# Experts of a routed layer as products of high and low parts, split tile by tile on ACT and DVE

## The reference

```python
x = L0_attn_hidden_states                      # 1 x 2048 x 512
x = x + L0_attn(layernorm(x))                  # Mamba-2 mixer, then a gated dense layer (2048 wide)
x = x + L0_ffn(layernorm(x))                   # routed experts

# _L0_ffn_ref: 8 experts of width 352, the 2 best of each row
probs = softmax(x @ Wr);  topk_w, topk_idx = top_k(probs, 2);  topk_w /= sum(topk_w)
g = einsum('bsh,ehi->besi', x, Wg)
u = einsum('bsh,ehi->besi', x, Wu)
h = silu(g) * u
y = einsum('besi,eih->besh', h, Wd)
out = einsum('bse,besh->bsh', combine, y)
```

## Time and profile before

| | us |
|---|---|
| median of 3 runs (lowest, highest) | 1515.2 (1514.8, 1515.47) |
| the profiled execution | 1515.05 |
| its span in the trace | 1513.3 |
| PE busy | 1439.8 |
| DVE busy | 782.0 |
| ACT busy | 446.9 |
| POOL busy | 431.4 |

### The profile page before, as it was taken

How to read it: one execution, slowest core, us unless ns; L and a number is a source line. 1 busy time by engine, 2 the same in 40 slices (tenths; PEclk the granted TensorE clock), 3 DMA queues, 4 the chain that set the end, 5 groups by cost and what they waited for, 6 DMA issues and landing times.

```text
span 1513.3 us, 19850 instructions
## 1 busy us (share of the span) xinstructions
PE 1439.8 (95%) x6903; PEld 1059.0 (70%) x6903; DVE 782.0 (52%) x1258; ACT 446.9 (30%) x927; POOL 431.4 (29%) x457
## 2 busy tenths in 40 slices
PE   6799999799999997999999999999988999999996
PEld 5577778566666666888888888888867655655663
DVE  6968787689999993332333333333468322222221
ACT  4445444545555553211111121112121111111110
POOL 2512121247777753111011011101010233332331
PEclk9899999999999999999999999999999999999998
DMA  9122223722233216001000000120377233333322
GB/s 197 56 92 103 85 84 132 209 91 98 105 113 125 98 57 209 28 15 43 14 28 23 19 28 14 48 70 0 109 249 247 45 61 66 67 59 67 61 40 34
DMA packets 84354, 124.41 MB, mean 82 GB/s; under 512 B 27695, under 2 KB 44079, under 8 KB 84272
## 3 DMA queue, kind: packets, MB, share of 16 engines
q1 hardware_dynamic: 71488, 103.62, 21.1%
q0 software_dynamic: 8736, 18.62, 7.2%
q10 hardware_dynamic: 4048, 1.10, 0.3%
HBM read 81.37 MB, written 43.78 MB: 83 GB/s over the span
## 4 chain that ended last, share of the span: by engine, by line
PE 59%; DVE 1%; DMA 1%; issue 0%; ACT 0%; POOL 0%; POOLq 0%; ACTq 0%; DVEq 0%
PE fin_bank L1797 35%; PE fin_bank L1938 12%; PE fin_bank L1958 6%; PE fin_bank L1928 1%; PE fin_bank L1907 1%; PE fin_bank L1947 1%; PE fin_bank L1920 0%; DMA out_dram<-result_rows,put_idx 0%; PE fin_bank L1865 0%; PE fin_bank L1853 0%; DMA xs<-xn_rows,idx 0%; PE fin_bank L1972 0%; DVE ff_w_lo L1593 0%; DVE fi_bn L1628 0%; ACT ff_w_hi L1517 0%
## 5 line engine op out<-in xcount | busy, mean ns | idle before, releaser
L1797 PE MATMUL fin_bank<-ff_hT_hi,ff_w_hi 128*128 128x512 f32 x512 | 202.6, 396 | 3.2 <-DVE ff_w_lo L1563 3.2
L1797 PE MATMUL fin_bank<-ff_hT_hi,ff_w_lo 128*128 128x512 f32 x512 | 202.4, 395 | 0.0
L1797 PE MATMUL fin_bank<-ff_hT_lo,ff_w_hi 128*128 128x512 f32 x512 | 202.4, 395 | 0.0
L1938 PE MATMUL fin_bank<-wx,xT 128*128 x624 | 192.8, 462 | 0.8 <-ACT xT L1532 0.8
L1555 DVE TENSOR_TENSOR ff_prod<-ff_prod,fin_bank 128x512 f32<-128x512 f32 x64 | 44.0, 688 | 263.1 <-PE fin_bank L1797 263.1
L1404 POOL TENSOR_TENSOR ff_w_lo<-ff_stage,ff_w_hi 128x1024 fp32r<-128x1024 f32 (+1 forms) x24 | 56.5, 2356 | 410.5 <-ACT ff_w_hi L1507 405.9
L1938 PEld LDWEIGHTS fin_bank<-wx,xT 128*128 128x128 f32 x624 | 116.3, 191 | 59.6 <-issue 2.5
L633 PE MATMUL pj_bank<-hT_hi,w_in_hi 128*128 128x512 f32 x336 | 136.9, 408 | 10.2 <-DVE zst L551 5.3
L533 DVE SCALAR_TENSOR_TENSOR conv_acc<-raw,conv_w,conv_acc 128x512 f32<-128x512 f32 x144 | 113.9, 791 | 45.0 <-ACT raw L339 37.4
L633 PE MATMUL pj_bank<-hT_lo,w_in_hi 128*128 128x512 f32 x336 | 134.5, 400 | 0.0
L633 PE MATMUL pj_bank<-hT_hi,w_in_lo 128*128 128x512 f32 x336 | 133.4, 397 | 0.0
(11 more groups left out here) (287 smaller groups left out, 2425.9 us busy)
## 6 DMA issues: line engine op xcount, KB each, us to landing
cv_rows<-cst SPq DMA_DIRECT2D x12, 1024.0 KB, 4.3
cv<-cv_rows SPq DMA_DIRECT2D x16, 768.0 KB, 4.3
zs_rows<-zst SPq DMA_DIRECT2D x8, 1024.0 KB, 6.5
zs<-zs_rows SPq DMA_DIRECT2D x16, 512.0 KB, 5.2
wx<-in_L_ffn_Wg_dram SPq DMA_DIRECT2D x8, 704.0 KB, 8.4
wx<-in_L_ffn_Wu_dram SPq DMA_DIRECT2D x8, 704.0 KB, 8.9
w_raw<-in_L_attn_in_proj_w_dram SPq DMA_DIRECT2D x32, 128.0 KB, 3.7
x<-_attn_hidden_states_dram SPq DMA_DIRECT2D x16, 256.0 KB, 5.5
```

Source lines behind the costliest of these rows:

```text
L1797: mm = eng.matmul(ps, w[a], x[b], start=first and i == 0, stop=last and i == 2)
L1938: mm = eng.matmul(ps[:, 0:EI], xT[j % 2][:, k, :], wx[:, bass.ds(e, 1), at:at + EI].rearrange("p a n -> p (a n)"), start=(k == 0), stop=(k ...
```

## The change

For the experts, gate and up use `three` for the first `KS` = 3 of their 4 blocks of 128 input features, and an fp32 product for the last; down uses `three` for all its blocks. The weights' parts are made anew for each tile: ACT copies the raw weights of the tile's expert to fp32r (`weights_high`), DVE subtracts that from the raw weights (`weights_low`). There is one buffer for each of gate, up and down, high and low. High parts of a tile may be written once PE has finished the same product of the tile before. Each of these instructions, on ACT and on DVE, first reads the expert's number (`owner`). The rows `xe` and the hidden values `he` are split in the same way, from PSUM. The scaling of the output rows moves from DVE to ACT. `wide` is called for gate and for up, with `turn_x` between. `turn_width` transposes three full blocks of 128 columns, with zeros behind the 352. POOL clears the padding of down's third block in `wx`, and clears `xs3` only after the second list of products.

At the end of PE's work in `project` stand 14 idle products of 128 columns.

```diff
                         turn_rows(g + 1, n - AT_TURN + 1)
+            for i in range(14):
+                eng.matmul(turn[1][:, 0:P], ones[:, :], ident[:, :], start=True, stop=True)
...
+        order = [("gate", 0), ("up", 0), ("gate", 1), ("up", 1)]
+        for j in range(SORT_TILES):
+            order += [("down", j)] + [(w, j + 2) for w in ("gate", "up") if j + 2 < SORT_TILES]
+        nth = {piece: i + 1 for i, piece in enumerate(order)}
+        ahead = {"gate": (wx, 0, KS * EI), "up": (wx, W_GU, KS * EI), "down": (wx, DN, NC * D)}
+        high = {"gate": gu_hi[:, 0, :], "up": gu_hi[:, 1, :], "down": wd_hi[:, :]}
+        low = {"gate": gu_lo[:, 0, :], "up": gu_lo[:, 1, :], "down": wd_lo[:, :]}
         block = ctx.enter_context(nc.Block())
+        def owner(eng, j):
+            return eng.value_load(tile_expert[0:1, j:j + 1], min_val=0, max_val=E - 1)
+        def raw_part(eng, kind, j):
+            t, at, n = ahead[kind]
+            return t[:, bass.ds(owner(eng, j), 1), at:at + n].rearrange("p a n -> p (a n)")
         def ge(eng, which, value):
...
+            eng.wait_ge(s["lgk"], NR * KD)
+            eng.wait_ge(s["rstd"], 3 * NR)
+            eng.memset(wx[EI % P:P, :, DN + (NC - 1) * D:DN + NC * D], 0.0).then_inc(s["const"], 1)
+            eng.wait_ge(s["const"], 12)
             for i in range(2):
                 eng.wait_ge(xn_dma[i], 16 * (NR // 2))
-            for t in xs:
-                eng.memset(t[:, :], 0.0).then_inc(s["cleared"], 1)
-            eng.wait_ge(s["cleared"], UN)
+            for t in xs[0:3]:
+                eng.memset(t[:, :], 0.0).then_inc(s["const"], 1)
+            eng.wait_ge(s["const"], 15)
...
+            def weights_high(kind, j):
+                done = {"gate": "eg_ps", "up": "eu_ps", "down": "y_ps"}[kind]
+                ge(eng, s[done], j)
+                eng.activation(high[kind], raw_part(eng, kind, j), ACT.Copy).then_inc(s["ew_hi"], 1)
             def turned(j):
                 eng.wait_ge(s["xT_ps"], j + 1)
                 ge(eng, s["eu_ps"], j - 1)
-                eng.activation(xT[j % 2][:, :, :].rearrange("p k n -> p (k n)"), xT_ps[:, :], ACT.Copy).then_inc(s["exT"], 1)
+                if KS < KD:
+                    eng.activation(xe_raw[j % 2][:, :], xT_ps[:, KS * P:KD * P], ACT.Copy)
+                eng.activation(xe_hi[j % 2][:, :, :].rearrange("p k n -> p (k n)"), xT_ps[:, 0:KS * P], ACT.Copy)\
+                   .then_inc(s["ex_hi"], 1)
             def gate(j):
                 eng.wait_ge(s["eg_ps"], j + 1)
                 ge(eng, s["hT_ps"], j - 1)
-                eng.activation(act_g[j % 2][:, :], eg_ps[j % 2][:, 0:EI], ACT.Silu).then_inc(s["esilu"], 1)
+                eng.activation(act_g[j % 2][:, 0:EI], eg_ps[j % 2][:, 0:EI], ACT.Silu).then_inc(s["esilu"], 1)
+            def width_high(j):
+                eng.wait_ge(s["hT_ps"], j + 1)
+                ge(eng, s["y_ps"], j - 1)
+                eng.activation(h_hi[j % 2][:, :, :].rearrange("p c n -> p (c n)"), hT_ps[:, 0:NC * P], ACT.Copy)\
+                   .then_inc(s["eh_hi"], 1)
+            def weighted(j):
+                eng.wait_ge(s["y_ps"], j + 1)
+                ge(eng, s["put"], 16 * (j - 1))
+                eng.activation(rows[j % 2][:, :], y_ps[j % 2][:, :], ACT.Copy, scale=wt[:, j:j + 1]).then_inc(s["sum"], 1)
+            eng.wait_ge(s["route"], R_TE)
+            eng.wait_ge(s["wx_dma"], 16 * 4 * E)
+            for i in range(2):
+                eng.wait_ge(xn_dma[i], 16 * (NR // 2))
+            weights_high("gate", 0)
+            weights_high("up", 0)
             turned(0)
             gate(0)
             turned(1)
+            weights_high("gate", 1)
+            weights_high("up", 1)
+            eng.wait_ge(s["const"], 12)
+            eng.wait_ge(s["table"], 2)
             for j in range(SORT_TILES):
+                weights_high("down", j)
+                width_high(j)
                 if j + 1 < SORT_TILES:
                     gate(j + 1)
                 if j + 2 < SORT_TILES:
                     turned(j + 2)
+                    weights_high("gate", j + 2)
+                if j:
+                    weighted(j - 1)
+                if j + 2 < SORT_TILES:
+                    weights_high("up", j + 2)
+            weighted(SORT_TILES - 1)
         @block.vector
         def _(eng):
@@ -1717,10 +1792,26 @@
             step(eng.tensor_reduce(te_f[:, :], cmp_t[:, :, :], AX_X, ALU.add))
             step(eng.tensor_scalar(te_f[:, :], te_f[:, :], float(E - 1), None, ALU.min))
             step(eng.tensor_copy(tile_expert[:, :], te_f[0:1, :]))
+            def weights_low(kind, j):
+                eng.wait_ge(s["ew_hi"], nth[kind, j])
+                eng.tensor_tensor(low[kind], raw_part(eng, kind, j), high[kind].bitcast(F32), ALU.subtract)\
+                   .then_inc(s["ew_lo"], 1)
+            def turned(j):
+                eng.wait_ge(s["ex_hi"], j + 1)
+                eng.tensor_tensor(xe_lo[j % 2][:, :, :].rearrange("p k n -> p (k n)"), xT_ps[:, 0:KS * P],
+                                  xe_hi[j % 2][:, :, :].rearrange("p k n -> p (k n)").bitcast(F32), ALU.subtract)\
+                   .then_inc(s["ex_lo"], 1)
+            weights_low("gate", 0)
             eng.wait_ge(s["table"], 1)
             eng.tensor_scalar(idx[:, :], table_ps[:, 0:SORT_TILES], float(ROWS), None, ALU.add).then_inc(s["ids"], 1)
             eng.tensor_copy(wt[:, :], table_ps[:, SORT_TILES:2 * SORT_TILES]).then_inc(s["ids"], 1)
             eng.wait_ge(s["ids"], 2)
+            for t in act_g:
+                eng.memset(t[:, EI:NC * P], 0.0)
+            weights_low("up", 0)
             def both_tiles(a):
                 return a.unsqueeze(1).broadcast_to([P, 2, E])
...
@@ -1766,28 +1858,30 @@
             def product(j):
                 eng.wait_ge(s["esilu"], j + 1)
                 eng.wait_ge(s["eu_ps"], j + 1)
-                eng.tensor_tensor(act_g[j % 2][:, :], act_g[j % 2][:, :], eu_ps[j % 2][:, 0:EI], ALU.mult).then_inc(s["eh"], 1)
-            def turned(j):
-                eng.wait_ge(s["hT_ps"], j + 1)
-                ge(eng, s["y_ps"], j - 1)
-                full = EI // P
-                n = EI - full * P
-                eng.tensor_copy(hT_e[:, j % 2, 0:full, :].rearrange("p c n -> p (c n)"), hT_ps[:, 0:full * P])
-                eng.tensor_copy(hT_e[0:n, j % 2, full, :], hT_ps[0:n, full * P:(full + 1) * P]).then_inc(s["hT"], 1)
-            def weighted(j):
-                eng.wait_ge(s["y_ps"], j + 1)
-                ge(eng, s["put"], 16 * (j - 1))
-                eng.tensor_scalar(rows[j % 2][:, :], y_ps[j % 2][:, :], wt[:, j:j + 1], None, ALU.mult).then_inc(s["sum"], 1)
+                eng.tensor_tensor(act_g[j % 2][:, 0:EI], act_g[j % 2][:, 0:EI], eu_ps[j % 2][:, 0:EI], ALU.mult)\
+                   .then_inc(s["eh"], 1)
+            def width_low(j):
+                eng.wait_ge(s["eh_hi"], j + 1)
+                eng.tensor_tensor(h_lo[j % 2][:, :, :].rearrange("p c n -> p (c n)"), hT_ps[:, 0:NC * P],
+                                  h_hi[j % 2][:, :, :].rearrange("p c n -> p (c n)").bitcast(F32), ALU.subtract)\
+                   .then_inc(s["eh_lo"], 1)
+            turned(1)
+            weights_low("gate", 1)
             product(0)
             put_list()
+            weights_low("up", 1)
             for j in range(SORT_TILES):
-                turned(j)
+                weights_low("down", j)
+                width_low(j)
+                if j + 2 < SORT_TILES:
+                    turned(j + 2)
                 if j + 1 < SORT_TILES:
                     product(j + 1)
-                weighted(j)
+                if j + 2 < SORT_TILES:
+                    weights_low("gate", j + 2)
+                    weights_low("up", j + 2)
         @block.tensor
         def _(eng):
@@ -1923,49 +2017,56 @@
             def turn_x(j):
                 eng.wait_ge(xs_s[j % UN], j // UN * 16 + 16)
-                ge(eng, s["exT"], j)
+                ge(eng, s["ex_lo"], j)
                 for k in range(KD):
                     last = eng.transpose(xT_ps[:, k * P:(k + 1) * P], xs[j % UN][:, k * P:(k + 1) * P], ident[:, :])
                 last.then_inc(s["xT_ps"], 1)
-            def wide(j):
-                e = eng.value_load(tile_expert[0:1, j:j + 1], min_val=0, max_val=E - 1)
-                eng.wait_ge(s["exT"], j + 1)
-                for i, (ps, free, done) in enumerate(((eg_ps[j % 2], "esilu", "eg_ps"), (eu_ps[j % 2], "eh", "eu_ps"))):
-                    ge(eng, s[free], j - 1)
-                    for k in range(KD):
+            def wide(j, kind):
+                i, ps, free, done = {"gate": (0, eg_ps[j % 2], "esilu", "eg_ps"), "up": (1, eu_ps[j % 2], "eh", "eu_ps")}[kind]
+                if i == 0:
+                    eng.wait_ge(s["ex_lo"], j + 1)
+                eng.wait_ge(s["ew_lo"], nth[kind, j])
+                ge(eng, s[free], j - 1)
+                for k in range(KS):
```

(38 more changed lines are left out.)

47 lines of the change are left out of this document (35 added, 12 removed).

## The result

The changed kernel takes 1606.97 us (median of 4 runs, 1606.5 to 1609.68) against 1515.34 for the one before (1514.8 to 1515.47); the ratio is 1.061, with a 95% interval of 1.0597 to 1.0623. I had forecast 1502.5 us, faster, and had put 1524 as the upper end. It is slower by 92 us.

What follows compares the result with a forecast made beforehand. PE's columns bound the kernel before; after, the down-weights loop would pace tiles at 7.68 us against 8.07. Terms: -14.4 + 3.4 - 0.15 - 0.3 - 1.2 = -12.6 us, from 1515.2 to 1502.5 us, range 1486 to 1524.

Steps and rivals of the forecast that it cites:

- The step that failed: Expert tiles, ACT's queue: scaling of output rows (0.60 us, formerly DVE's 0.75) behind the gate weights would hold nobody.
- The loop of the down weights: Expert tiles: from down's end through ACT's copy, DVE's subtraction and two reads to next down's end, 7.68 us, setting the pace.
- The last tile: Last expert tile, down(38): it now also waits for the whole 7.68 us loop, +3.4 us.
- PE's own work: Expert tile on PE after the change: transposes, gate, up and down together 6.93 us, before 8.07.
- The queues: ACT and DVE, 5.9 us a tile each: fit in 7.68 only if their other two reads run during computing.
- Rival B: Expert tiles: reads do not run ahead, all three in DVE's time, 8.3 us a tile, 1525 us; chance 22%.
- Rival C: Expert tiles: a draw, waiting reads take 489 ns and not 300, loop 8.06 us, time 1517 us; chance 10%.
- POOL's clearing: Clearing of the padding, in POOL's 16 us of idle time before the gathers: claimed to cost nothing.
- The start of the experts: Before the first tiles: extra DVE subtractions, PE's first gate later but shorter; -0.3 us, bounds -1.5 and +2.5.
- The idle products: End of the projection: 14 products keep PE's clock full over the following gap; -1.2 us, bounds -3 and +0.3.
- the two rules that I weighed: Skill pages: register reads take at least about 600 ns; two-SBUF-input DVE subtractions contend with GpSimd, up to 2.6 us a tile.
- Slower: Outcome that the changed kernel takes longer than before, by reads falling in DVE's own time; chance 0.22.

Runs made afterwards that it cites:

- e2: Changed kernel with one move on POOL: the gather of tile j+4, not j+3, stands ahead of the put of tile j; 1505.55 us, ratio 0.9933.
- f1: Kernel before, expert products still fp32, with only the scaling of the result rows moved from DVE to ACT; 1540.0 us, ratio 1.0154.
- f2: e2's kernel with the expert-number reads on ACT and DVE moved ahead of the semaphore waits; 1480.83 us, ratio 0.977.
- g3: Changed kernel with gather one tile earlier, reads ahead of the waits and POOL's clearing behind the last norm; 1477.05 us, ratio 0.9747.
- f3: e2's kernel with the down product back in fp32 from the raw weights, no high and low copies; 1496.62 us, ratio 0.9871.
- e4: Kernel before with only POOL's clearing of the padding, beside DVE's last norm as in the changed kernel; 1520.17 us, ratio 1.0026.
- e3: Kernel before with only the 14 idle products at the end of the projection; 1513.22 us, ratio 0.9986.
- f4: e2's kernel with POOL's clearing of the padding behind the last norm instead of beside it; 1502.05 us, ratio 0.9908.

## Why the prediction was wrong

**The step that failed** is the sentence "On ACT the scaling of the output rows ... stands behind the gate weights and holds nobody". I had asked of it only whether ACT has the time. It holds POOL's put, the put stands ahead of the gather of tile j+3 in POOL's queue, and that gather feeds the turned rows which stand ahead of the next scaling on ACT. Before, DVE scaled right behind the down product, so the gather left early and the same POOL order was harmless. The step is worth 37 x (10.36 - 7.57) = 103 us, and the whole miss is 104; e2 shows it, and f1 shows it without the rest of the change. In the 103 are also what the circle's steps gained by the change itself, the longer puts (37 x 0.42 = 16 us, estimated) and the transposes at the lower clock. Each of its large steps stood in the trace of before or in my own terms: the put's issue, the gather, the transposes (0.67), the copies on ACT. I never added them up.

**The loop of the down weights**, 7.68 forecast, was right where it rules: 7.58 in the changed kernel's first tile, 7.57 in e2. Term by term in e2's chain against the earlier trace rows: down with PE's end 2.37 (2.30), the read on ACT 0.66 (0.75), copy 1.50 (1.46), the read on DVE 0.77 with the handover (0.79), subtraction and hidden low part 2.24 (2.23), DVE to PE 0.04 (0.15). The wait before down was put down to `he_lo`, as said, but PE's engine was idle for 0.44 in the mean there (15.7 us in 36 tiles of e2) and not for 0.7.

**The last tile**, +3.4 forecast, was +3.8 in the changed kernel, and 7.56 - 4.21 = +3.35 in e2. I had left out that the clock is at its lower level behind the wait before it: down(38) took 4.22 and not 2.10. The stretch from its start to the end was 0.7 longer in the changed kernel; I had put -0.15.

**PE's own work**, 6.93, is 7.00 in f2 and g3, 7.44 in f3 (I had derived 7.41). Products of 352 columns follow one another by 0.16, as taken.

**The queues.** Rival B had all three reads of each engine in DVE's own time; its 8.3 did not come. Rival C's slow reads exist (see the last section) but not as a rule: e2's loop is 7.57.

**POOL's clearing** "costs nothing" was the second sentence that failed: 3.5 us. It lies in POOL's idle time, but it holds up an instruction of DVE which stands on the chain. I had checked only whose time it takes, and not beside whom it runs.

**The start of the experts**: forecast -0.3 (bounds -1.5 and +2.5), measured +4.9 up to the first transposes of gathered rows and +1.0 from there to down(0). Of the +4.9 the clearing is 3.5 (e4: 595.83 against 592.31). Another 1.17 lies in the first gather, 4.78 from issue to landing against 3.61. Most of that is the issue itself, 2.39 against 1.33, and a subtraction of weights on DVE had begun 0.08 before it. No run took that subtraction away, so the cause is not shown by an experiment, but it is the pattern of the puts.

**The idle products**, -1.2: e3 gives -2.1 (-0.8 to -3.5), and the two traces -2.8 and -2.95. Right in kind, and on the small side.

Of the two rules that I weighed, neither gives the circle. The floor for reads was not borne out: the median is 278 ns on ACT and 308 on DVE, below the 600 that the Trainium skill's page "DMA: Bandwidth & Descriptors", section "Latency and other measured facts", gives. The second I set aside by a wrong reading of the earlier trace rows. I looked only at DVE's instruction, which kept its 0.80; the longer instruction is POOL's. That gather's issue took 1.63 us, and of the 39 of the kernel before only the first (1.33) and this one took over 1.07. So a subtraction of weights, of which the change puts three into each tile, had to be weighed against POOL's puts and gathers; the changed kernel's puts are longer where one runs beside them.

As for the rivals, I had three and all of them were about the engines' loads. "Slower" had 0.22 by a mechanism that did not occur. What I had forecast is the time of the change without the two faults: f4, which has neither, took 1502.05 against 1502.5. That the two lie within 0.5 us is luck. Against the trace of the kernel before, f4's steady tiles gave -16.0 (I had put -14.4), the start to the dense layer -3.2 (-1.2), the start of the experts up to down(0) +2.8 (-0.3), the last tile +3.35 (+3.4) and the end +0.55 (-0.15).

## What to carry to other kernels

When an operation moves to another engine, ask not only whether that engine has time but who waits for its result, what is queued behind that waiter, and whether any of it comes back to something ahead of the operation in its new queue: write the circle down with the durations of each step and divide by the number of tiles that it spans. A circle that spans one tile is cut as well by widening its lead (here one gather earlier, 101 us) as by moving the operation. A register read in front of the work, whose value is ready long before, goes ahead of the semaphore wait, and an instruction in an engine's idle time is free only if it holds up no instruction of the chain that runs beside it.
